# Eigenvalue search: GpSimd multiplies the older of a row's two rows, and VectorE's second operation is a plain sum

## The reference

```python
deg = jnp.sum(A, axis=0) + jnp.sum(A, axis=1) - jnp.diagonal(A)
d_inv_sqrt = jnp.where(deg > 0, jax.lax.rsqrt(deg), 0.0)
L = jnp.diag(deg) - A
L_norm = d_inv_sqrt[:, None] * L * d_inv_sqrt[None, :]
_, U = jnp.linalg.eigh(L_norm)
agg = jnp.einsum('mn,bnd->bmd', U.T, features)
h = jax.nn.relu(agg @ W1 + b1)
out = h @ W2 + b2
return jnp.einsum('nm,bmd->bnd', U, out)
```

## Time and profile before

| | |
|---|---|
| median of 3 runs | 9420.81 us (9412.58 to 9423.52) |
| the profiled execution | 9429.72 us |
| its span | 9428.0 us |
| VectorE busy in the span | 6835.7 us |
| GpSimd busy in the span | 1158.8 us |

### The profile page before, as it was taken

How to read it: one execution, slowest core, us unless ns; L and a number is a source line. 1 busy time by engine, 2 the same in 40 slices (tenths; PEclk the granted TensorE clock), 3 DMA queues, 4 the chain that set the end, 5 groups by cost and what they waited for, 6 DMA issues and landing times. The chain is left out here.

```text
span 9428.0 us, 329059 instructions
## 1 busy us (share of the span) xinstructions
PE 5999.5 (64%) x137424; PEld 4052.0 (43%) x137424; DVE 6835.7 (73%) x32993; ACT 2558.8 (27%) x7301; POOL 1158.8 (12%) x5161
## 2 busy tenths in 40 slices
PE   5695888777878787777777777434333330036956
PEld 2364555555666666556666655101000000033446
DVE  3566666776777877777777777888888889964055
ACT  1441111111111111111111112466656560010046
POOL 0000111111222222222222222000000000000000
PEclk8898999999999989877665555555555555569989
DMA  1000000000000000000000000000000000000000
GB/s 37 1 1 20 4 4 4 4 4 4 4 4 4 4 4 4 4 4 4 4 4 4 4 3 3 1 0 0 0 0 0 0 0 0 0 0 0 1 19 19
DMA packets 24643, 42.56 MB, mean 5 GB/s; under 512 B 2464, under 2 KB 20128, under 8 KB 23200
## 3 DMA queue, kind: packets, MB, share of 16 engines
q1 hardware_dynamic: 23200, 21.70, 0.7%
HBM read 17.50 MB, written 4.19 MB: 2 GB/s over the span
## 5 line engine op out<-in xcount | busy, mean ns | idle before, releaser
L289 PE MATMUL tri_y<-L 128*32 128x256 f32 (+7 forms) x36792 | 1946.6, 344 | 9.6 <-issue 7.9
L289 PEld LDWEIGHTS tri_y<-L 128*32 128x32 f32 x36792 | 1202.5, 122 | 222.8 <-issue 45.1
L1398 PE MATMUL ev_pairs<-ev_sgn,ident 128*128 128x448 bf16 x1024 | 428.6, 574 | 675.5 <-ACT ev_sgn L1363 675.5
L364 ACT ACTIVATE tri_mu<-tri_ring,tri_tiny 128x1 f32<-128x1 f32 x1022 | 267.4, 262 | 2154.8 <-PE tri_ring L272 2154.8
L366 ACT ACTIVATE tri_sM<-tri_half_M,tri_s 128x8 f32<-128x8 f32 (+7 forms) x1022 | 304.2, 298 | 1832.2 <-DVE tri_s L468 1832.2
L314 PE MATMUL tri_ring<-ident 128*128 128x128 bf16 x7414 | 750.3, 268 | 1.1 <-issue 1.0
L272 PE MATMUL tri_k<-tri_kp,tri_half 128*32 128x1 f32 x8176 | 264.5, 189 | 763.0 <-DVE tri_x L476 759.6
L1507 DVE SCALAR_TENSOR_TENSOR ev_seq<-ev_seq,ev_rowG,ev_u 128x112 f32<-128x112 f32 x2048 | 685.4, 335 | 80.9
L314 PEld LDWEIGHTS tri_ring<-ident 128*128 128x128 bf16 x7414 | 582.2, 121 | 170.9 <-issue 155.1
L1502 DVE TENSOR_TENSOR ev_u<-ev_shifted,ev_seq 128x112 f32<-128x112 f32 x2048 | 561.9, 274 | 111.8 <-DVE ev_seq L1517 17.4
L272 PEld LDWEIGHTS tri_k<-tri_kp,tri_half 128*32 128x32 f32 x8176 | 177.4, 120 | 1044.3 <-DVE tri_x L476 1043.0
(11 more groups left out here) (616 smaller groups left out, 13390.1 us busy)
## 6 DMA issues: line engine op xcount, KB each, us to landing
adj<-in_adj_dram SPq DMA_DIRECT2D x12, 1024.0 KB, 8.2
x<-in_x_dram SPq DMA_DIRECT2D x8, 512.0 KB, 7.2
out_dram<-x SPq DMA_DIRECT2D x8, 512.0 KB, 6.6
gcn_w<-in_L_gnn_W_dram SPq DMA_DIRECT2D x2, 128.0 KB, 2.1
spec_w<-in_L_gnn_W_dram SPq DMA_DIRECT2D x2, 64.0 KB, 1.8
dot_wt<-in_L_gnn_W_dram SPq DMA_DIRECT2D x1, 64.0 KB, 1.7
dot_rows<-in_L_gnn_b_lin_dram SPq DMA_DIRECT2D x1, 64.0 KB, 2.8
dot_rows<-in_L_gnn_b_dram SPq DMA_DIRECT2D x1, 64.0 KB, 3.7
```

Source lines behind the costliest of these rows:

```text
L289: last = nc.tensor.matmul(y[32 * g:32 * g + 32, 0:T * 32], A[:, b + t, XC:XC + 1].broadcast_to([P, 32]), cols, start=(t == 0), stop=(t == ...
L364: nc.scalar.activation(mu[:, :], sigma, ACT.Sqrt, bias=tiny[:, :]).then_inc(root_ready, 1)
L1398: last = nc.tensor.matmul(sums[h], S["ident16"][:, :], sgn[:, h * (GRP // 2) + k:(h + 1) * (GRP // 2) + k, :].rearrange("p s w -> p (s w)" ...
```

## The change

The product of the older row with minus the square moves from VectorE to GpSimd. GpSimd writes it to a new tile `past[:, s]`, one slot for each of the eight rows of a group, as `seq[:, z, s] * rowG[:, z, 1, s]`, and counts `past_ready`. VectorE's second operation of a row becomes the sum of `past[:, s]` and `u`, and waits for `past_ready` besides its wait on `chain`. GpSimd waits on `chain` until the older row is written: for the rows s = 0 and s = 1 until the end of the group before (a count of 19 for each group before), for later rows until the sum of row s - 2. The first product of each eight groups is written as a product of two tensors, one of them broadcast. A small memset on VectorE at the head of each turn of the loop counts `opened`, for which GpSimd waits before it goes on to the counts of a new turn, and VectorE clears `past_ready` beside `chain` at its end.

```diff
+            for q in range(NPASS):
+                with pool.Fori(0, NG // PACK) as it:
+
+                    pool.wait_ge(opened, it + (q * (NG // PACK) + 1))
+                    for y in range(PACK):
+                        for s in range(GRP):
+
+                            at = y * (2 * GRP + 3) + 2 * (s - 1) if s else y * (2 * GRP + 3)
+                            if y == 0 and s == 0:
+                                nc.gpsimd.tensor_tensor(past[:, s, :], seq[:, 0, 0, :], rowG[:, 0, 1, 0:1].broadcast_to([P, W]), ALU.mult).then_inc(past_ready, 1)
+                                continue
+                            if at:
+                                pool.wait_ge(chain, at)
+                            nc.gpsimd.tensor_scalar(past[:, s, :], seq[:, y % 2, s, :], rowG[:, y % 2, 1, s:s + 1], None, ALU.mult).then_inc(past_ready, 1)
...
+                    V.memset(dummy[:, 0:1], 0.0).then_inc(opened, 1)
                     ready = 0
...
-                            ready = mark(V.scalar_tensor_tensor(out=seq[:, z, s + 2, :], in0=seq[:, z, s, :], scalar=rowG[:, z, 1, s:s + 1], in1=u[:, :],
-                                                                op0=ALU.mult, op1=ALU.add))
+                            dve.wait_ge(past_ready, y * GRP + s + 1)
+                            ready = mark(V.tensor_tensor(seq[:, z, s + 2, :], past[:, s, :], u[:, :], ALU.add))
...
                     dve.sem_clear(range(chain.num, chain.num + 1))
+                    dve.sem_clear(range(past_ready.num, past_ready.num + 1))
```

More of the change, by code:

```diff
@@ L1308, in eigenvalues @@
         x = sb("x", [P, B, PTS]); lo = sb("lo", [P, B]); base = sb("base", [P, 1])
-        rowH = sb("rowH", [P, NG + 2, 2, GRP]); rowG = sb("rowG", [P, 2, 2, GRP]); shifted = sb("shifted", [P, 2, GRP, W])
+        rowH = sb("rowH", [P, NG + 2, 2, GRP]); rowG = sb("rowG", [P, 2, 2, GRP]); shifted = sb("shifted", [P, 2, GRP, W]); past = sb("past", [P, GRP, W])
         seq = sb("seq", [P, 2, GRP + 2, W]); sgn = sb("sgn", [P, GRP + 1, W], BF16); same = sb("same", [P, GRP, W], BF16)
@@ L1323, in eigenvalues @@
         dummy = sb("dummy", [P, 2])
-        setup, chain, tables, seq_ready, sgn_done, pass_ready, shifted_ready, summed, same_ready, ends_ready, swapped, middle_ready, signs_ready, halves_ready, folded, grid_ready, \
+        setup, chain, tables, seq_ready, sgn_done, pass_ready, shifted_ready, summed, same_ready, opened, past_ready, ends_ready, swapped, middle_ready, signs_ready, halves_ready, folded, grid_ready, \
             spread_ready, evens, odds, idx_ready, idx_swapped, row_done = map(
-                sem, ("setup", "chain", "tables", "seq_ready", "sgn_done", "pass_ready", "shifted_ready", "summed", "same_ready", "ends_ready", "swapped", "middle_ready", "signs_ready",
+                sem, ("setup", "chain", "tables", "seq_ready", "sgn_done", "pass_ready", "shifted_ready", "summed", "same_ready", "opened", "past_ready", "ends_ready", "swapped", "middle_ready", "signs_ready",
                       "halves_ready", "folded", "grid_ready", "spread_ready", "evens", "odds", "idx_ready", "idx_swapped", "row_done"))
```

## The result

The changed kernel is slower: 9474.8 us, median of 4 runs (9470.3 to 9487.5), against 9417.6 us before in 4 runs; the ratio is 1.0063, 95% interval 1.0045 to 1.008. The forecast was 9379 us and faster. The time lies inside the stated range of 9350 to 9640 us, which was drawn wide for the slower rivals; the sign is wrong.

What follows compares the result with a forecast made beforehand. The chain through VectorE was taken to bound the eigenvalue search. Saving 125 us, plus 78 for group-start stalls and 5 for loop turns, gave -42 us: 9379 us against the median, likeliest 9353 to 9405, eight in ten 9350 to 9640.

Steps and rivals of the forecast that it cites:

- What the second operation saves: VectorE's second operation of each row: a sum replaces the multiply-add, 61 ns less over 2048 rows, 125 us saved.
- The loop turns: At each of 32 loop turns: an added memset and semaphore clear on VectorE, 0.15 us each, 5 us in all.
- The gap in the middle of a group: Inside a group: GpSimd may take 0.78 us, needs 0.50, so products of seven rows in eight are hidden.
- Rival 3: In every row: GpSimd becomes the clock at 0.72 us per row, 9640 us; chance 0.11.
- The stall at the group start: Before each group's first sum: VectorE waits 0.305 us for GpSimd, 256 times, 78 us (52 to 104).
- T + 0.65: Group start: GpSimd delivers the first product 0.10 + 0.50 + 0.05 us after T, the end of the instruction writing the older row.
- the additional wait in row 3: Fourth row of a group: its extra wait for ScalarE was taken to cost nothing, the step being 0.31 us like others.
- No disturbance between the engines: In each row: VectorE and GpSimd both reading SBUF were forecast to slow each other by near zero.
- c: Disturbance per row between VectorE and GpSimd: forecast near zero, upper case 93 ns, break-even 20 ns (42 us over 2048 rows).
- the small tiles: Evidence from the earlier trace: operations of 6 to 12 elements on both engines overlapped without waiting for each other's whole instruction.
- Rival 2: In each row: reads collide and the sum waits for GpSimd's stream; 93 ns gives 9569 us, 36 ns 9453; chance 0.24.
- Rival 4: In every row: whole VectorE and GpSimd instructions exclude each other, a row takes 1.155 us, 10,400 us; chance 0.07.

Runs made afterwards that it cites:

- sum_alone: Kernel before with VectorE's multiply-add replaced by the plain sum, the multiplication left out and GpSimd idle; 9284.2 us, ratio 0.9858.
- half_width: Changed kernel with GpSimd's product on 56 of the 112 elements only, the other half left at zero; 9385.1 us, ratio 0.9957.
- u_in_psum: Changed kernel with the product u kept in PSUM, so VectorE's sum has one SBUF input; 9413.0 us, ratio 0.9994.
- sum_bystander: bystander_read with VectorE's multiply-add replaced by the plain sum, the multiplication left out; 9375.2 us, ratio 0.9955.
- from2: Changed kernel with the multiply-add of rows 0 and 1 of each group kept on VectorE, GpSimd making rows 2 to 7; 9381.7 us, ratio 0.9966.
- tt_product: Changed kernel with GpSimd's product written as a two-tensor product with a broadcast operand in every row; 9455.5 us, ratio 1.0033.
- bystander_read: Changed kernel, but VectorE keeps its multiply-add and GpSimd's per-row product reads unchanging tiles into a tile nobody reads; 9439.2 us, ratio 1.0018.

## Why the prediction was wrong

**What the second operation saves: right.** 125 us were forecast, and sum_alone shows 132 by the medians and 123 by the busy time of the line (685.4 - 562.4).

**The loop turns: right.** 5 us were forecast, and the memset and the product's shorter wait make 5.0 together.

**The gap in the middle of a group: right.** No row but the first waits for GpSimd, with all eight products or with six. Rival 3, GpSimd as the stage's clock, did not come: its 0.65 us fits in the 0.655 us of a row, with nearly nothing to spare. The sign that I named for it, no idle time between GpSimd's operations, did show (eight in 5.12 us), so it was a poor sign: GpSimd can be busy without a gap while each product is still ready before its sum.

**The stall at the group start: right in place, too small in size.** 78 us were forecast; the idle time before the sum rose by 112.5 us. T + 0.65 was to be the moment of the first sum. In the group of the timeline T is 6026.18, and the sum starts at 6027.03, T + 0.85. GpSimd starts at T + 0.10, as forecast. Its operation takes 0.65 us, not 0.50, and from its end to the sum are 0.10 us, not 0.05. Of the 0.15 us, 0.06 is my choice of the middle between 2.75 and 0.83 ns per element, where half_width gives 2.55. The other 0.09 us are VectorE's: GpSimd's operations last 558 ns where no product of VectorE is ahead of them and 646 ns where one is, so this part of the stall is a collision too. In the later passes the first product starts at T + 0.12 in place of T + 0.03, in the kernel before as well, so that the idle time before the sum is 0.45 us there and not 0.53. The small part of the idle time that VectorE itself ends (19.3 us over 97 times, by the list of waits) is the additional wait in row 3, which was not free in the later passes (the sum that starts late there keeps its 274 ns); the kernel before has it too, by a smaller amount. I read one group of the first pass only, and saw neither.

**No disturbance between the engines: wrong, and this is the step that turned the sign.** I put c near zero "because VectorE's product finishes its reading before GpSimd's data is far advanced". It is the sum that is hit, and GpSimd is pushed towards it by the product. Measured, the sums are longer by 37 ns in six rows and by 79 in the first: 635.6 us of busy time against 2048 x 274 ns = 561 us is 75 us more, above the break-even of 42. Term by term, -125 + 78 + 5 + 0 = -42 was forecast, and -125 + 112.5 + 5 + 75 = +68 came. The stall's error alone would have left the sign as it was (-7); the disturbance alone would have turned it (-42 + 75 = +33). u_in_psum, where the sums are not disturbed and the stall stays, comes out at 9413 us, near no change.

Two things said ahead of the result need a correction. That the engines meet only at semaphores holds for their order, not for their time: in sum_bystander no semaphore joins a sum to GpSimd, and it is longer. And the small tiles against which I weighed the disturbance could not have shown it: L430 inside L254 has one input tile in its row, and L469 beside L256 is a multiply-add, the form that from2 shows unchanged at 0.25 us behind GpSimd. The rows to look for were those of a plain two-tensor operation beside GpSimd.

Rival 2 named this mechanism, with 93 ns as its price and 9569 us, and 9453 us at 36 ns; the price came out at 75 us / 2048 = 37 ns, and the longer stall makes the rest. My reading is that part of GpSimd's reading falls where VectorE does not read; the durations fit it, and no run measures the reads themselves. Rival 4, whole instructions that exclude each other, is refuted by the first sum of a group: it starts at 6027.03 while GpSimd's operation of 0.56 us (6026.90) is under way, and ends at 6027.38, ahead of it.

```profile
6026.90 0.56 POOL L1357 TENSOR_SCALAR ev_past<-ev_seq,ev_rowG 128x112 f32<-128x112 f32 x1
6027.03 0.35 DVE L1523 TENSOR_TENSOR ev_seq<-ev_past,ev_u 128x112 f32<-128x112 f32 x1 [0.53 <-POOL ev_past L1357]
```

**How long the hold lasts.** Three situations agree on one figure, one is near it, and one with half of the elements shows a shorter one. It is counted from GpSimd's start to the point at which VectorE's instruction would have had to start to be left alone. Row 0 of the changed kernel: started 0.12 us behind GpSimd and 0.08 late, 0.20. sum_bystander: 0.17 behind and 0.04 late, 0.21.

```profile
6028.56 0.56 POOL L1357 TENSOR_SCALAR ev_past<-ev_flat,ev_kth 128x112 f32<-128x112 f32 x1
6028.73 0.31 DVE L1522 TENSOR_TENSOR ev_seq<-ev_seq,ev_u 128x112 f32<-128x112 f32 x1
```

Rows 1 to 6 of the changed kernel: 0.25 behind and 0.04 late is 0.29, with GpSimd itself held up by 0.09: again 0.20. tt_product, the other form of GpSimd's operation: the product 0.05 behind and 0.19 late, 0.24. half_width: 0.13 behind and 0.02 late is 0.15, with half of the elements. Here is row 1 of the changed kernel:

```profile
6027.41 0.28 DVE L1517 TENSOR_TENSOR ev_u<-ev_shifted,ev_seq 128x112 f32<-128x112 f32 x1
6027.47 0.65 POOL L1357 TENSOR_SCALAR ev_past<-ev_seq,ev_rowG 128x112 f32<-128x112 f32 x1
6027.73 0.31 DVE L1523 TENSOR_TENSOR ev_seq<-ev_past,ev_u 128x112 f32<-128x112 f32 x1
```

The 0.05 us between 112 and 56 elements make 0.9 ns each, near the copy's 0.83 of the earlier trace rows. That would fit a GpSimd that fetches its input at that rate, however long it then computes. It rests on two lengths and is not measured by itself, and at 0.9 ns each 112 elements make 0.10 us: the other 0.10 of the hold has no explanation here.

The Trainium skill, SBUF — State Buffer, section Who interferes with whom, says that two SBUF inputs on VectorE contend with a GpSimd instruction that reads SBUF, not with one that only writes it. The runs agree for the plain sum and the product: 306 ns beside a reader with two SBUF inputs, 271 with one of the two in PSUM, and 335 and 275 unchanged beside the memset. The same section of the Trainium skill says that the issue order decides who blocks. tt_product fits (0.46 us against 0.27), but in the later passes of the changed kernel GpSimd starts 0.03 us ahead by its record and is the one that is held up. By the section SBUF: two separate sides of the same page of the Trainium skill, whoever starts first has the shared pair for the whole instruction and the other fully blocks. The runs differ: VectorE was free 0.20 us after the start of an operation of 0.56 us. I gave the rule with its full length (rival 4) 0.07 and a shorter collision (rival 2) 0.24, on the small tiles alone; the collision deserved far more.

## What to carry to other kernels

Before work moves to an idle GpSimd beside a VectorE chain, look at the SBUF inputs on both sides: here a plain two-tensor VectorE operation with both in SBUF was held up by a GpSimd operation that reads SBUF (37 to 79 ns), and held GpSimd up in turn (88 ns). Rows of another form of operation, or of a few elements, say little about it: look for the form and the number of inputs that the change will have. Putting one operand in PSUM removed what VectorE lost. And look for the one item of a loop that has no lead: here the first row behind each group turn gave back most of the gain, and leaving that row and the next on VectorE turned +57 us into -38 (from2 against its own runs of before).

## What the runs showed of the hardware

- GpSimd's tensor_scalar with a per-partition scalar took 558 ns at 112 elements and 415 at 56, 2.55 ns per element; the same product written as two tensors with a broadcast operand took 367 ns unhindered and 462 behind a VectorE product.
- A VectorE sum with two SBUF inputs was 37 to 79 ns longer beside it; a multiply-add with a scalar, 0.25 us behind GpSimd's start as the sums are, kept its 335 ns (from2). Its additional 61 ns may come ahead of its data; that is not shown. Where GpSimd started 0.05 us behind the multiply-add, in 23 of 2048 places of bystander_read, it took 0.35 to 0.36 us.
- VectorE wrote the product to PSUM in 283 ns in place of 275 and read it back in 271 in place of 275: 8 - 4 = 4 ns for a pair, against the 37 ns a row that the conflict cost.
- ScalarE did the same product in 387 ns; a VectorE product with two SBUF inputs that lay wholly beside it kept its 0.27 us.
